# A linear attention's key sums, outputs and norms in another order: two query rotations moved, the outputs added and normed by halves

## The reference

```python
QKV = X @ W_in + b_in;  Q, K, V = split(QKV)         # 2 sequences of 1024 tokens, 256 features
Q, K = rope(Q), rope(K)                              # first 128 features rotated in pairs
A = sum_over_sequence(K / |K| * V)                   # one vector of 256 per sequence
Y = (A * Q) @ W_out + b_out;  x = x + Y + norm(x)    # norm(x) is the attention's X
# FFN: 32 experts, 6 of them per token
scores = sigmoid(norm(x) @ gate);  w = top6(scores) / sum
x = x + 0.5 * (sum_over_top6(w * expert(norm(x))) + shared(norm(x)))
```

## Time and profile before

| | |
|---|---|
| median of 3 runs | 1303.91 us (1302.14 to 1304.94) |
| span of the profiled execution | 1495.7 us |
| PE busy, weight loads beside it | 1178.6 us (79%), 960.0 us |
| DVE busy | 743.8 us (50%) |
| ACT busy | 536.0 us (36%) |
| POOL busy | 596.8 us (40%) |

### The profile page before, as it was taken

One profiled execution on the slowest core, in us unless ns is written; L12 is line 12 of the kernel. 1 busy time (PEld: TensorE's weight loads), 2 busy tenths in 40 slices (PEclk: granted clock), 3 DMA queues, 4 the chain that ended last, 5 costly groups with the idle time before them and its releaser, 6 DMA issues.

```text
span 1495.7 us, 20198 instructions
## 1 busy us (share of the span) xinstructions
PE 1178.6 (79%) x6031; PEld 960.0 (64%) x6031; DVE 743.8 (50%) x2333; ACT 536.0 (36%) x1012; POOL 596.8 (40%) x579
## 2 busy tenths in 40 slices
PE   4799988979989898854768998897755436988884
PEld 4677755666778676633557987875434225978784
DVE  5553465564546536413445555678644214633443
ACT  2323344554533234321413433442303115644442
POOL 3661352211124213674550155662453730045554
PEclk9789999998989999865868999898875667998897
DMA  9523439400002573331426687760121212676676
GB/s 331 211 72 107 143 96 308 141 1 0 1 29 107 206 260 119 117 114 64 173 76 216 195 241 237 219 191 4 60 79 41 105 53 63 198 208 205 204 223 191
DMA packets 125302, 209.81 MB, mean 140 GB/s; under 512 B 15296, under 2 KB 104768, under 8 KB 123328
## 3 DMA queue, kind: packets, MB, share of 16 engines
q1 hardware_dynamic: 100624, 141.38, 28.7%
q0 software_dynamic: 24576, 67.14, 14.4%
HBM read 129.29 MB, written 101.19 MB: 154 GB/s over the span
## 4 chain that ended last, share of the span: by engine, by line
PE 48%; DVE 18%; issue 13%; another core or an unknown queue 10%; ACT 6%; POOL 3%; DMA 1%; SPq 0%; DVEq 0%; POOLq 0%; ACTq 0%
PE ps L910 15%; PE ps L932 6%; PE ps L877 5%; PE ps L817 4%; PE ps L829 4%; PE ps L889 3%; PE ps L1093 2%; PE ps L1100 2%; ACT xnt L1360 1%; PE ps L927 1%; PE ps L1244 1%; DVE HL L2047 1%; POOL xd L638 1%; PE ps L925 1%
## 5 line engine op out<-in xcount | busy, mean ns | idle before, releaser
L653 POOL DMA_INDIRECT G<-yd,slot_of x256 | 253.1, 989 | 424.6 <-issue 189.3
L638 POOL DMA_INDIRECT xd<-xnt,slot_of x256 | 251.4, 982 | 224.4 <-DVE slot_of L1986 136.9
L910 PE MATMUL ps<-WE,xT 128*128 x1016 | 200.7, 343 | 5.6 <-issue 3.9
L2102 DVE TENSOR_TENSOR hid<-hid,ps 128x192 f32<-128x192 f32 (+2 forms) x168 | 65.4, 389 | 247.9 <-ACT hid L1551 198.1
L910 PEld LDWEIGHTS ps<-WE,xT 128*128 128x128 f32 x1016 | 174.0, 202 | 9.9 <-issue 9.7
L1522 ACT ACTIVATE xT<-ps 128x512 f32<-128x512 f32 (+1 forms) x168 | 99.2, 590 | 156.9 <-PE ps L877 121.6
L877 PE MATMUL ps<-ident,xd_in 128*128 128x128 f32 x664 | 108.2, 287 | 44.2 <-ACT xT L1522 24.0
L2081 DVE SCALAR_TENSOR_TENSOR XT<-G,wt,XT 128x256 f32<-128x256 f32 x256 | 123.8, 494 | 27.5 <-DMA G<-yd,slot_of 17.0
L1551 ACT ACTIVATE hid<-ps 128x192 f32<-128x192 f32 (+2 forms) x168 | 60.4, 359 | 192.1 <-PE ps L910 139.9
L877 PEld LDWEIGHTS ps<-ident,xd_in 128*128 128x128 f32 x664 | 84.5, 148 | 60.6 <-issue 37.0
L1379 ACT ACTIVATE S<-ps 128x512 f32<-128x512 f32 (+1 forms) x72 | 42.6, 592 | 179.1 <-PE ps L817 140.1
(11 more groups left out here) (245 smaller groups left out, 2173.6 us busy)
## 6 DMA issues: line engine op xcount, KB each, us to landing
xd_in<-xd SPq DMA_DIRECT2D x164, 256.0 KB
yd<-yo SPq DMA_DIRECT2D x164, 256.0 KB
WE<-w SPq DMA_DIRECT2D x8, 1280.0 KB
W0E<-w0e SPq DMA_DIRECT2D x1, 4864.0 KB
xd<-xnt,slot_of POOLq DMA_INDIRECT x256
G<-yd,slot_of POOLq DMA_INDIRECT x256
W0E<-w0e SPq DMA_DIRECT2D x1, 3040.0 KB
XT<-x_in SPq DMA_DIRECT2D x4, 512.0 KB, 6.1
```

The source lines that it names most:

```text
L638: nc.gpsimd.indirect_dma_start(xd[f // 2][:, :], bass.IndirectOffsetOnAxis(ap=slot_of[:, t, k:k + 1], axis=0), xnt[:, t, :], None).then_in ...
L653: nc.gpsimd.indirect_dma_start(G[:, n % G_RING, :], None, yd[f // 2][0:min(ly.early[t][k] * 2, ly.TILES) * P, :], bass.IndirectOffsetOnAxi ...
L910: last = mm(dst, xT[:, q % 2, a, k, :], flat[:, bass.ds(expert[2 * q + a] + k * 2 * ly.H, 2 * ly.H)], start=(k == 0), stop=(k == KD - 1))
L2102: tt(hid[:, q % 2, 0:m, 0:ly.H], hid[:, q % 2, 0:m, 0:ly.H], src, ALU.mult).then_inc(TL.hid, 1)
```

## The change

Four edits, none of which changes what is computed:

1. `key_sums` needs only the values (v2), not the rotation of q1, and stands ahead of it in all four groups; in a half's second group `weighted` does too.
2. `project_out` writes its pieces to banks `OUT_BANK` and waits for the queries of each group by itself, so that its first two pieces need only the first group's.
3. `summed(b)` adds and norms by pieces: add two tiles, their statistics, the next two, then variance. The order of DVE is block 0, then the attention's norm of block 3 (`last_stats`), then block 1. On ACT the attention's rows of block 3 go behind block 0's score.
4. `turn` takes the tiles one after the other and waits for each tile's rows, in all 29 turns of the program.

Lines of the changed kernel are the old ones plus 1 from L310 and plus 2 from about L1250.

```diff
-TAKEN = {"k1": 3, "v1": 4, "v2": 5, "q1": 8, "rn": 10}
+TAKEN = {"k1": 3, "v1": 4, "v2": 5, "rn": 7, "q1": 10}
...
+        OUT_BANK = (0, A_BANK, 1, 2)
...
             def turn(norm, b, src, bank):
-                pe.wait_ge(norm.rows, NT * (b + 1))
-                for k in range(KD):
-                    for a in range(NT):
+                for a in range(NT):
+                    pe.wait_ge(norm.rows, NT * b + a + 1)
+                    for k in range(KD):
...
                     elif s:
-                        pe.wait_ge(A1.add, n + 1)
+                        pe.wait_ge(A1.add, (1, 3, 4, 4)[n])
...
             def project_out(s):
                 pe.wait_ge(A1.wo, s + 1)
-                pe.wait_ge(A1.qrot, 2 * s + 2)
-                pe.wait_ge(A1.q2, 2 * s + 2)
                 for h in range(ST // 2):
+                    if h % 2 == 0:
+                        pe.wait_ge(A1.qrot, 2 * s + 1 + h // 2)
+                        pe.wait_ge(A1.q2, 2 * s + 1 + h // 2)
                     for i in range(2):
...
-                        dst = ps[:, h, i * D:(i + 1) * D]
+                        dst = ps[:, OUT_BANK[h], i * D:(i + 1) * D]
...
-                std(AT_NORM, 3)
-                rows(AT_NORM, 3, XT[:, tiles_of(3), :])
                 flipped(2, B_BANK)
                 std(F_NORM[3], 0)
                 rows(F_NORM[3], 0, XT[:, tiles_of(0), :])
+                std(AT_NORM, 3)
                 std(F_NORM[3], 1)
                 plain(0)
                 split_high(0)
                 score(3, 0, A_BANK + 1)
+                rows(AT_NORM, 3, XT[:, tiles_of(3), :])
                 rows(F_NORM[3], 1, XT[:, tiles_of(1), :])
...
             def key_sums(g):
...
-                dve.wait_ge(A1.taken, TAKES * g + TAKEN["q1"])
+                dve.wait_ge(A1.taken, TAKES * g + TAKEN["v2"])
...
+            def summed(b):
+                s = b // 2
+                for i in range(2):
+                    h = 2 * (b % 2) + i
+                    added(s, h)
+                    dve.wait_ge(A1.add, 4 * s + h + 1)
+                    for a in (2 * i, 2 * i + 1):
+                        last = nc.vector.bn_stats(st6[:, a, :], XT[:, b * NT + a, :])
...
+                for a in range(NT):
+                    last = nc.vector.bn_aggr(mv[:, b * NT + a, :], st6[:, a, :])
...
+                ts(rs[:, 0, tiles_of(b)], mv[:, tiles_of(b), 1], EPS, None, ALU.add).then_inc(F_NORM[3].var, 1)
...
+                key_sums(0)
                 rotated(0, "q1", QT[:, 0, 0, :], A1.qrot)
-                key_sums(0)
...
-                rotated(1, "q1", QT[:, 1, 0, :], A1.qrot)
                 key_sums(1)
                 weighted()
+                rotated(1, "q1", QT[:, 1, 0, :], A1.qrot)
+                summed(0)
+                offsets(F_NORM[f], 0, True)
                 last_stats()
                 offsets(AT_NORM, 3, True)
-                added(0, 0)
-                added(0, 1)
-                dve.wait_ge(A1.add, 2)
-                stats(F_NORM[f], 0, XT[:, tiles_of(0), :])
-                added(0, 2)
-                offsets(F_NORM[f], 0, True)
-                added(0, 3)
-                dve.wait_ge(A1.add, 4)
-                stats(F_NORM[f], 1, XT[:, tiles_of(1), :])
+                summed(1)
                 offsets(F_NORM[f], 1, True)
```

More of the change, by code:

```diff
@@ L2480, in key_sums @@
                         accum_out=apart[:, k, g % 2:g % 2 + 1]).then_inc(A1.taken, 1)
-                dve.wait_ge(A1.taken, TAKES * (g + 1))
+                dve.wait_ge(A1.taken, TAKES * g + TAKEN["rn"])
             def weighted():
@@ L2492, in added @@
                 dve.wait_ge(A1.y, 4 * s + h + 1)
-                tt(rows, rows, ps[:, h, :], ALU.add).then_inc(A1.add, 1)
+                tt(rows, rows, ps[:, OUT_BANK[h], :], ALU.add).then_inc(A1.add, 1)
+            def summed(b):
[6 more added lines that the diff above has]
+                        last = nc.vector.bn_stats(st6[:, a, :], XT[:, b * NT + a, :])
+                st.do(last)
+                st.sync()
+                for a in range(NT):
+                    last = nc.vector.bn_aggr(mv[:, b * NT + a, :], st6[:, a, :])
+                st.do(last)
+                st.sync()
+                ts(rs[:, 0, tiles_of(b)], mv[:, tiles_of(b), 1], EPS, None, ALU.add).then_inc(F_NORM[3].var, 1)
             def split_low(b):
@@ L2573, in window @@
                 key_inverse(2)
+                key_sums(2)
                 rotated(2, "q1", QT[:, 0, 0, :], A1.qrot)
-                key_sums(2)
                 chosen(f, 1)
@@ L2580, in window @@
                 key_inverse(3)
-                rotated(3, "q1", QT[:, 1, 0, :], A1.qrot)
                 key_sums(3)
                 weighted()
+                rotated(3, "q1", QT[:, 1, 0, :], A1.qrot)
                 dve.wait_ge(A1.res, 2)
[L2585 to L2589, removed]
+                summed(2)
                 offsets(F_NORM[f], 2, True)
-                added(1, 3)
-                dve.wait_ge(A1.add, 8)
-                stats(F_NORM[f], 3, XT[:, tiles_of(3), :])
+                summed(3)
                 offsets(F_NORM[f], 3, True)
```

## The result

The changed kernel takes 1304.23 us (median of 22 runs, 1297.85 to 1311.27), the kernel before 1302.05 in as many runs beside it. The ratio is 1.003, 95% interval 1.0016 to 1.0044: 2 to 6 us slower, 3.9 by the ratio and 2.2 by the two medians, where 3.7 was forecast.

A forecast was written before the change was run, and what follows sets the result against it. The prediction took the moment block 0's slots are written, followed by POOL's 96 unbroken scatters, as setting the end. Terms 0 + 4.7 - 1.0 = +3.7 us on 1303.91 gave 1307.6 us, range 1298.9 to 1312.5.

The forecast's parts named there:

- What bounds the kernel: Last layer's window: POOL's 96 scatters run without a stop, 121.5 us from when block 0's slots are written.
- The stalls of the disturbed profile: Long DVE waits inside POOL's scatter bursts, 8.34 to 32.93 us, in the 1495.7 us profile; mostly absent from plain runs.
- the last rival: Stalls are in plain runs too and block 2's slots set the end: 1308.6 us, chance 0.05.
- Key sums first: DVE waits 1.36 us in group 0; group 1's sums start 0.9 later; taking the rotation out gains half a microsecond.
- Halves, and what is late next: Block 0's rows on ACT begin 1.5 us earlier, but block 1's root delays the copy; the gains are used up.
- The zero: Sum of all terms up to block 0's score, expected at 1051.6 against 1051.71: no net change.
- The moved rows and POOL's additions: Behind block 0's score, POOL's two residual adds hold two DVE instructions of the expert choice: 4.7 us later.
- The first rival: POOL waits instead of DVE, so 4.7 becomes 1.3 for the later ranking: 1304.2 us, no change, chance 0.30.
- Turns elsewhere: Row-wise turns ahead of the window, counted in the second layer-0 tile loop: gain of 1.0 us.
- The faster rival: Row-wise turns pay at all seven places ahead of the window: 1300.7 us, chance 0.25.
- Second pair of blocks: Block 1's slots come some 3 us later; cost 0, or 3 if the cover is gone.
- the cover: POOL still has scatters of block 0 to start when block 1's slots come, so their delay costs nothing.

The follow-up runs named there:

- before_again: The kernel before, unchanged, profiled and timed again for a profile without the long stalls; ratio 1.0013 to the kernel before.
- res3_dve: The changed kernel with block 3's residual additions made by DVE behind the key inverse of group 2, none by POOL there; ratio 1.0004 to the kernel before.
- adds_twice: The changed kernel with two more POOL additions (of zero) behind the two of block 3; ratio 1.0056 to the kernel before.
- turn_only: The kernel before with only the row-wise turn, which waits for each tile's rows; ratio 1.0011 to the kernel before.
- late_norm: The changed kernel with group 0's sums behind the rotation again, block 3's residual additions on DVE and its attention norm later; 1296.93 us, ratio 0.9965.
- late_norm_old_turn: late_norm with the old turn, which waits once for all rows; ratio 0.9976 to the kernel before.

## Why the prediction was right, point by point

Six rows of the changed kernel's timelines (DVE, PE and ACT) and five of before_again (PE and DVE) are used here beside those above:

```profile
936.47 0.69 DVE L2481 SCALAR_TENSOR_TENSOR TA<-KB,ps 128x512 f32<-128x512 f32 x1 [3.84 <-PE ps L1238]
...
956.06 7.17 PE L1258 MATMUL ps<-WSH,QT 128*128 128x256 f32 x32 [1.37 <-DVE WSH L2489]
...
962.94 0.16 DVE L1858 SCALAR_TENSOR_TENSOR rs<-mv,rs 128x4 f32<-128x4 f32 x1
...
969.12 0.20 ACT L1356 ACTIVATE rs<-rs 128x4 f32<-128x4 f32 x1 [3.82 <-DVE rs L2511]
969.23 1.01 ACT L1751 ACTIVATE G<-ps 128x1024 f32<-128x1024 f32 x1
...
972.47 0.28 ACT L1375 ACTIVATE sc<-ps 128x128 f32<-128x128 f32 x1
```

```profile
952.26 10.13 PE L1256 MATMUL ps<-WSH,QT 128*128 128x256 f32 x32 [3.90 <-DVE WSH L2487]
...
956.08 0.69 DVE L2493 TENSOR_TENSOR XT<-XT,ps 128x512 f32<-128x512 f32 x1 [1.29 <-PE ps L1256]
...
958.97 0.69 DVE L2493 TENSOR_TENSOR XT<-XT,ps 128x512 f32<-128x512 f32 x1 [2.21 <-PE ps L1256]
...
961.54 0.24 DVE L1849 TENSOR_SCALAR rs<-mv 128x4 f32<-128x4 f32 x1
...
962.49 0.16 DVE L1856 SCALAR_TENSOR_TENSOR rs<-mv,rs 128x4 f32<-128x4 f32 x1
```

- **What bounds the kernel.** Right: POOL's train of 96 writes, 121.16 us where 121.5 was worked out, from the slots of block 0. The stalls of the disturbed profile were rightly left out, and the last rival, which has them in plain runs too, is out with them.
- **Key sums first.** The mechanism was right, both sizes wrong. DVE waits 3.84 us for group 0's broadcast, not 1.36: the number came from the disturbed trace, where DVE had waited 2.06 us for a value product and came late to the rotation. In group 1 the broadcast ends 2.63 us later (30.53 from the start of S against 27.90), not 1.36; but before, the sums began 2.57 behind it, not half a microsecond, because the rotation stood between. The two cancel, and the weights come 0.09 later instead of 0.8.
- **Halves, and what is late next.** Block 0's offset ends 3.25 us earlier from the start of S (962.94 + 0.16 - 923.28 = 39.82 against 962.49 + 0.16 - 919.58 = 43.07), not 1.5, and not for the reason given. POOL's additions held the offsets for 1.71 us in the disturbed profile; in before_again the offsets take 0.16 and the variance ahead of them 0.24. What went is DVE's wait for PE's outputs, 1.29 and 2.21 us: PE idles 1.37 us ahead of them instead of 3.90 and makes them in 7.17 us instead of 10.13, and the rotation lies under them. The 3.25 is used up: ACT's root of block 1 (969.12) holds the copy (969.23), as forecast. But the score still comes 0.66 earlier than before (49.19 from the start of S against 49.85), and DVE reaches the choice 0.07 later, 1.1 behind it. So DVE is the late one, and from the weights to the choice it needs 17.87 us against 17.89: the rotation of 3.0 came in where 3.5 of waits went. The zero was right, but as the sum of terms that the text had otherwise; that is luck in part.
- **The moved rows and POOL's additions.** The term that carries the result. Predicted 4.7, measured 4.0: 3.40 of held instructions and 0.6 of a slower ranking. The mechanism was right. The text took both additions whole, but the mask came 1.0 us into the first one; the slower ranking it did not have (and six small instructions follow the mask, not seven, on which nothing rests). Res3_dve and adds_twice show the cause from both sides. The first rival (POOL waits) is out, and its price of 1.3 for the later ranking measured 1.0 (res3_dve).
- **Turns elsewhere.** -1.0 is not borne out: S of turn_only and before_again is the same and the time shows no gain, though by its interval 0.7 us can't be excluded. The faster rival needed 5.7 us and is out.
- **Second pair of blocks.** The slots of block 1 come 24.93 us after those of block 0 (1012.09 - 987.16) against 22.68, 2.25 later where 3 was said, and the cover held.

The sum, 0.07 + 3.4 + 0.6 = 4.1 us, is so close to 3.7 by luck: two terms were too large in opposite directions, by 0.7 and 1.0. That the kernel gets slower, and by what, was not luck: the held instructions are there as forecast.

## What to carry to other kernels

Before moving a GpSimd elementwise instruction, list which small VectorE instructions will run beside it: here each such one that was held took as long as what was left of the GpSimd one, and on a chain of sub-microsecond steps that outweighed what the reordering gained. Take a wait as worth its microseconds only after asking which engine comes next and whether it is free then: here 11 us of PE's waits went and no time could be seen with them, and in the window read here DVE was the late one. If a profile's span is far from the plain times, have it taken again before sizing terms from it.

## What was not expected of the hardware

PE's granted clock in one short stretch differs between runs of the same instructions in the same order. In the five microseconds that hold the products of group 1 (q1, q2) it is 1.00 in before_again and 0.66 in turn_only, a mixture of the two levels of 2.4 and 1.2 GHz; PE had idled 1.41 us ahead of the norm products in front of it in both. The windows of before_again and of turn_only:

```profile
942.58:947.58 5.00, 5.00 (x23) 2.87 (x23) 4.52 (x11) 0.86 (x2) 0.00 (x0) 1.00 0.00 0
```

```profile
944.53:949.53 5.00, 5.00 (x12) 2.22 (x12) 4.52 (x11) 0.17 (x1) 0.00 (x0) 0.66 0.00 0
```

Over all profiles with group 0's sums behind the rotation the eight products took 3.81 us once, 5.38 four times and 6.45 once; with the sums first, where PE idles 2.03 us at an earlier place instead, 3.82 in all five. Between late_norm and late_norm_old_turn this moved S by 1.66 us, between before_again and turn_only by nothing, so a difference of a microsecond or two between single profiles can be the clock's. The outputs (32 matmuls) go with PE's idle time ahead of them: 7.17 us in the eight profiles with 1.37 us of it, where the granted clock over them is 1.00, 8.86 in the two with 2.33 or 2.34 (0.81), and 10.13 in the one with 3.90 (0.70).

And an instruction with one SBUF operand can be held as well: the mask (L1923, a comparison of one tensor) took 1.43 us beside POOL's addition, while the reciprocal and the match instructions ahead of it, which ran beside the same addition (from 974.85 on), kept their 0.2. The Trainium skill (SBUF — State Buffer, section "Who interferes with whom") names such scalar operations among those that can take the shared ports, so the trace agrees.
